# The rotary halves by a shuffle instead of a second projection, and the first prototype step inside the perceptron's slots

## The reference, cut to what matters

```
# L0: self attention with rotary q and k, cross attention, perceptron, each gated
x_norm = _ln(x, norm1_w) * (1 + sc_msa) + sh_msa
q, k, v = x_norm @ qkv_W            # 16 heads of 8 features
q, k = t * cos + rot(t) * sin       # rot(t) = concat([-t2, t1]) of a head's two halves
x = x + g_msa * (attn(q, k, v, mask) @ attn_out_W)
x = x + g_x * cross_attention(x, ctx);  x = x + g_mlp * mlp(x)
# L1: routed experts over prototypes
nx = layernorm(x) * gamma + beta
weights = softmax((nx @ Wq) @ (ctx @ Wk).T / sqrt(128))
evidence = weights @ (ctx @ Wv)
probs = softmax([nx, evidence, cond] @ router_W + router_b)
x = x + sigmoid(gate) * (sum_e probs_e * expert_e([nx, evidence, cond]) @ out_w + out_b)
# L2: cross attention; L3: self attention, cross attention, perceptron
```

## Time and profile before

| | |
|---|---|
| median of 3 runs | 1156.64 us (1152.13 to 1156.79) |
| profiled execution | 1156.29 us |
| its span in the trace | 1154.5 us |
| granted TensorE clock, mean | 0.966 |
| busy: PE, DVE, POOL, ACT | 1054.8, 783.1, 653.4, 574.2 us |
| instructions | 28612 |

### The profile page before, as it was taken

One profiled execution on the slowest core, in us unless ns is written; L12 is line 12 of the kernel. 1 busy time (PEld: TensorE's weight loads), 2 busy tenths in 40 slices (PEclk: granted clock), 3 DMA queues, 4 the chain that ended last, 5 costly groups with the idle time before them and its releaser, 6 DMA issues.

```text
span 1154.5 us, 28612 instructions
## 1 busy us (share of the span) xinstructions
PE 1054.8 (91%) x11711; PEld 665.8 (58%) x11711; DVE 783.1 (68%) x1875; ACT 574.2 (50%) x803; POOL 653.4 (57%) x762
## 2 busy tenths in 40 slices
PE   7899999999998997999899879999999999999898
PEld 4445555556654775666556545665555556665476
DVE  6677777777884433666667878878888777777321
ACT  1034444456656563544435336666556566665553
POOL 5476666677785331121112579888677665577531
PEclk8799999999999997999999979999999999999899
DMA  4300000000000112000000000000000000000001
GB/s 177 130 2 2 11 20 12 11 20 21 11 20 20 37 37 86 6 12 6 6 6 12 11 7 7 2 2 2 2 2 1 2 2 2 2 2 3 1 28 46
DMA packets 9281, 22.89 MB, mean 20 GB/s; under 512 B 1392, under 2 KB 1648, under 8 KB 8768
## 3 DMA queue, kind: packets, MB, share of 16 engines
q1 hardware_dynamic: 9152, 21.07, 5.5%
HBM read 18.90 MB, written 2.15 MB: 18 GB/s over the span
## 4 chain that ended last, share of the span: by engine, by line
PE 67%; DVE 19%; issue 6%; ACT 4%; POOL 3%; DMA 0%; DVEq 0%; POOLq 0%; ACTq 0%
PE weighed L646 11%; DVE negmax L1121 10%; PE row_scores L588 6%; PE scores L792 6%; PE weighed L669 5%; PE scores L619 5%; PE scores L545 4%; PE row_scores L792 3%; PE quads L529 3%; PE quads L552 2%; PE quads L540 2%; ACT p L1527 2%; PE scores L659 2%; PE scores L631 2%; DVE hat L1077 2%
## 5 line engine op out<-in xcount | busy, mean ns | idle before, releaser
L1121 DVE TENSOR_REDUCE negmax<-row_scores 128x8 f32<-128x616 f32 (+1 forms) x312 | 300.6, 964 | 83.7 <-PE row_scores L588 61.2
L1527 ACT ACTIVATE p<-scores 128x1024 f32<-128x1024 f32 (+1 forms) x256 | 247.6, 1018 | 214.9 <-PE scores L631 214.9
L619 PE MATMUL scores<-qblk,work 32*77 32x512 f32 (+1 forms) x1280 | 204.8, 616 | 10.5 <-ACT p L1527 5.8
L1679 POOL TENSOR_TENSOR kblk_r<-work,pack_const 128x308 fp32r<-128x308 f32 (+1 forms) x160 | 133.8, 837 | 119.5 <-PE row_scores L588 101.2
L588 PE MATMUL row_scores<-kblk_r,qr 32*128 32x308 f32 (+1 forms) x624 | 140.5, 439 | 40.0 <-DVE negmax L1121 39.0
L646 PE MATMUL weighed<-p,v 77*32 77x128 f32 (+1 forms) x5120 | 174.3, 277 | 2.5 <-DVE nat L1137 2.5
L1669 POOL TENSOR_TENSOR qblk<-work,pack_const 128x512 f32<-128x512 f32 x160 | 166.1, 1038 | 0.0
L646 PEld LDWEIGHTS weighed<-p,v 77*32 77x32 f32 (+1 forms) x5120 | 131.1, 110 | 46.2 <-issue 42.8
L631 PE MATMUL scores<-nblk,select 32*77 32x512 f32 (+1 forms) x640 | 155.3, 799 | 0.0
L588 PEld LDWEIGHTS row_scores<-kblk_r,qr 32*128 32x128 f32 x624 | 63.0, 187 | 158.2 <-issue 73.2
L1137 DVE STREAM_TRANSPOSE nat<-weighed 128x256 f32<-128x256 f32 x160 | 71.1, 444 | 45.1 <-PE weighed L646 45.1
(11 more groups left out here) (294 smaller groups left out, 1846.9 us busy)
## 6 DMA issues: line engine op xcount, KB each, us to landing
shared<-gates_hbm SPq DMA_DIRECT2D x24, 256.0 KB, 3.3
shared<-in_ctx_tok SPq DMA_DIRECT2D x16, 154.0 KB
pack_w_l<-in_w_l SPq DMA_DIRECT2D x1, 2058.5 KB, 10.9
x<-in_x_tok SPq DMA_DIRECT2D x8, 256.0 KB, 6.5
out_x<-x SPq DMA_DIRECT2D x8, 256.0 KB, 2.0
layers_w<-in_w_l SPq DMA_DIRECT2D x1, 1289.0 KB, 9.2
ctxT<-in_ctxT SPq DMA_DIRECT2D x1, 1232.0 KB, 9.1
layers_w<-in_w_l SPq DMA_DIRECT2D x1, 640.0 KB, 6.0
```

The costliest lines, as they stand in the source:

```text
L619: mm = e.matmul(scores[0:nk, g, :], k_of[q % 3][at, s * nk:(s + 1) * nk], qblk[n % 2][at, :], start=layer.mask != "qk", stop=False, skip_g ...
L1121: e.tensor_reduce(negmax[q % 2][:, 2 * h:2 * h + 2, 0, s * NJ:(s + 1) * NJ], row_banks(n, h)[:, :, 0:NJ * nk].rearrange("p g (j k) -> p g ...
L1527: e.activation(p[n % 2][0:nk, 8 * h:8 * h + 8, :], scores[0:nk, 2 * h:2 * h + 2, :].rearrange("p g (j q) -> p (g j) q", j=NJ), ACT.Exp, bi ...
L1679: e.tensor_tensor(kblk_r[n % 2][:, 0:NJ * nk].rearrange("p (j k) -> p j k", j=NJ), k_of[q % 3][:, s * nk:(s + 1) * nk].unsqueeze(1).to_bro ...
```

## The change

**Rotation.** The swapped projections and their weights go. `rotate` takes the cosine product from `quad_bank` first, then copies `quad_bank` with the two halves of each head exchanged into `rot` by `stream_shuffle` (partition i reads partition i xor 4, within 32). POOL's `add_rotated` multiplies `rot` by the sine in place, and then adds. PE's waits for the swapped result are gone.

**First prototypes.** The chain of quad 0 leaves `routed()` and gets places in the tail slots 11 to 17 of phase 0 on PE, DVE and ACT. `routed_x(0)` and `routed_x(1)` on POOL stand in slots 11 and 15, the former ahead of `add_perceptron`; quad 1's keys are projected in slot 17. The context tokens of quad 0 get a tile of their own (`ctx_first`), loaded early. The perceptron's temporary is moved out of `p[0]`, and `routed()` begins at i = 1.

```diff
-                if layer.rope:
-                    w.wait_ge(exp_done, early)
-                    e.matmul(scores[:, 1, :], W["l0_qswap"], xn[q % 3], start=True, stop=True).then_inc(proj_swapped, 1)
                 e.matmul(quad_bank[:, :], W[layer.wq], xn[q % 3], start=True, stop=True).then_inc(proj_q, 1)
...
-                w.wait_ge(proj_swapped, 2 * q + which + 1)
-                e.tensor_tensor(by_seq(rot[which][:, :]), by_seq(scores[:, 1, :]),
-                                sin_live[:, live:live + 1, :].to_broadcast([128, QUAD, S]), ALU.mult).then_inc(rope_half, 1)
-                w.wait_ge(proj, q + 1)
                 e.tensor_tensor(by_seq(dst), by_seq(quad_bank[:, :]),
                                 cos_live[:, live:live + 1, :].to_broadcast([128, QUAD, S]), ALU.mult).then_inc(rope_half, 1)
+                w.wait_ge(rope_done, 2 * (q - 1) + which + 1)
+                e.stream_shuffle(rot[which][:, :], quad_bank[:, :], [i ^ (HD // 2) for i in range(TILE)]).then_inc(rope_half, 1)
...
                 w.wait_ge(rope_half, 4 * q + 2 * which + 2)
+                e.tensor_tensor(by_seq(rot[which][:, :]), by_seq(rot[which][:, :]),
+                                sin_live[:, which:which + 1, :].to_broadcast([128, QUAD, S]), ALU.mult).then_inc(rope_turned, 1)
+                w.wait_ge(rope_turned, 2 * q + which + 1)
                 e.tensor_tensor(dst, dst, rot[which][:, :], ALU.add).then_inc(rope_done, 1)
...
+            def first_prototypes(slot):
+                if slot == 11:
+                    w.wait_ge(exp_done, 16 * NB)
+                    w.wait_ge(wo_read, 2 * NB)
+                    w.wait_ge(fold_done, FOLDING)
+                    project_keys(0)
+                if slot == 12:
+                    turn_nx(0)
+                if slot == 13:
+                    prototype_scores(0)
+                if slot == 14:
+                    turn_weights(0)
+                if slot == 15:
+                    w.wait_ge(ln_done, A_NORMS)
+                    evidence(0)
+                if slot == 17:
+                    evidence_logits(0)
+                    project_keys(1)
...
+                        if t == 4 * hi + 13:
+                            softmax_max(0)
+                            softmax_divide(0)
+                        if t == 4 * hi + 17:
+                            routed_stats(2)
+                            router_max(0)
...
+            def first_prototypes(slot):
+                if slot == 11:
+                    take_keys(0)
+                if slot == 12:
+                    take_nx(0)
+                if slot == 14:
+                    e.preload_act_table_set("natural_log_exp_and_others")
+                    w.wait_ge(r_sub, 1)
+                    e.activation(weights[0], weights[0], ACT.Exp).then_inc(r_exp, 1)
+                    routed_root(1)
+                    take_weights(0)
+                if slot == 15:
+                    take_evidence(0)
+                if slot == 17:
+                    take_keys(1)
...
-            for i in range(NB + 2):
+            for i in range(1, NB + 2):
```

More of the change, by code:

```diff
@@ L266, in build @@
               + [p_ for p_, _ in PACKS] + [f"x{c}" for c in range(NB)]
-              + [f"g{i}" for i in range(2)] + [f"ctx_tok{i}" for i in range(3)]}
+              + [f"g{i}" for i in range(2)] + ["ctx_first"] + [f"ctx_tok{i}" for i in range(3)]}
         pack_of = {name: p_ for p_, items in PACKS for name, _ in items}
@@ L459, in build @@
         mlp_banks, mlp_out_bank = [scores[:, 2, :], scores[:, 3, :], row_scores[:, 0, :], row_scores[:, 1, :]], av_bank[:, :]
-        mlp_t = [four(i, 0) for i in range(2)]
+        mlp_t = [four(1, i) for i in range(2)]
         def tensor_program(e):
@@ L520, in xn_ready, with project_q @@
                     w.wait_ge(ln_done, NORM_OF[layer.name, q].index + 1)
-            def project_q(q, early):
+            def project_q(q):
                 layer = layer_of(q)
@@ L536, in project_k @@
                     w.wait_ge(ld["ctx"], 16)
-                if layer.rope:
-                    w.wait_ge(exp_done, early)
-                    e.matmul(scores[:, 1, :], W["l0_kswap"], kv_source(q), start=True, stop=True).then_inc(proj_swapped, 1)
                 e.matmul(quad_bank[:, 0:QUAD * layer.nk], W[layer.wk], kv_source(q), start=True, stop=True).then_inc(proj_k, 1)
@@ L732, in quad_work @@
                     if cl == 3 and qi + 3 in quads:
-                        project_q(qi + 3, early)
+                        project_q(qi + 3)
                 for t in range(4 * lo + first, end):
@@ L772, in attention @@
                         turn_max(qi + 1)
+                    if phase == 0 and last is None:
+                        first_prototypes(t - 4 * hi)
                     if t == -10:
@@ L874, in routed @@
             def routed():
[L876 to L878 removed]
                 w.wait_ge(mlp_act, 4 * NB)
                 w.wait_ge(mlp_read, NB)
[L881 to L883 removed]
+                for i in range(1, NB + 1):
                     c, m = i - 1, i - 2
@@ L1402, in output_biases @@
                 done.then_inc(bias_done, 1)
-            w.wait_ge(mlp_added, NB)
-            for i in range(NB + 1):
+            for i in range(1, NB + 1):
                 c, m = i - 1, i - 2
@@ L1559, in mlp_hidden @@
-            def mlp_hidden(phase, c, hi):
-                func, bias, in_done, out_done, act_done = (
-                    (ACT.Gelu_apprx_tanh, "l0_b1", mlp_in, mlp_out, mlp_act), (ACT.Gelu, "l3_b1", ffn_in, ffn_out, ffn_act))[phase]
-                w.wait_ge(scores_done, 4 * hi)
-                for f in range(4):
-                    w.wait_ge(in_done, 4 * c + f + 1)
-                    w.wait_ge(out_done, c - 1)
-                    e.activation(mlp_h[c % 2][f], mlp_banks[f], func, bias=W[bias][:, f:f + 1]).then_inc(act_done, 1)
@@ L1833, in sync_program @@
             w.wait_ge(mlp_delta, NB)
-            for use in range(2 * NB):
+            for use in range(1, 2 * NB):
                 if use == 3:
```

178 lines of the change are left out of this document (91 added, 87 removed).

## The result

| | before | after |
|---|---|---|
| median | 1155.18 us (4 runs, 1152.13 to 1156.79) | 1138.43 us (4 runs, 1136.52 to 1139.70) |
| profiled execution, span | 1156.29, 1154.5 us | 1136.52, 1134.7 us |
| granted clock, mean | 0.966 | 0.967 |
| busy PE, DVE, POOL, ACT | 1054.8, 783.1, 653.4, 574.2 us | 1039.2, 782.1, 673.5, 571.8 us |

What follows compares the result with a forecast made beforehand. PE was taken to bound the rotary and perceptron slots, with a bare chain behind them. Rotary slots -9.6, lead -0.5 and routed start -12.6 sum to -22.7 us on 1156.29: 1133.6 us, range 1127 to 1144.

Steps and rivals of the forecast that it cites:

- Start of the routed stage: After the perceptron: quad 0's bare prototype chain, moved into perceptron slots, finds cover and the hidden layer's clock rises; -12.6 us.
- 0.78 us absorbed: Ahead of the last second layer: logits and second keys fill PE's wait for DVE, cutting moved work from 4.4 to 3.6 us.
- the hidden layer at full clock: Start of the routed stage: the first hidden layer's four records take 1.72 us instead of 3.08, another 1.4 us gained.
- Swapped projections: Rotary slots: eleven projections removed from PE, five q and six k, each worth 0.96 us; 10.6 us in all.
- DVE late by 0.20 us in each q slot: Rotary slots: the shuffle ends after PE is ready, in five q slots, giving 1.0 us back.
- Lead: Before the first slot: later spread of k against q projections saved; -0.5 us, with 3 us either way.
- The first spread of k: In the lead, where PE waits on it: POOL's two added multiplications less an earlier start cost +1.5 us.
- The two later q projections: In the lead, at half clock: their removal brings -1.1 and -0.9 us after POOL and DVE take some back.
- POOL as the bound: Rival, chance 0.12: POOL bounds the rotary slots, so only 1 us of the 9.6 is won; 1142.2 us.
- chain stalled in the slots: Rival, chance 0.08: the prototype chain stalls in perceptron slots, two waits of 3.54 us laid bare; 1140.7 us.
- the clock in the lead: Rival, chance 0.06: with five projections fewer in the lead, PE's clock rises two slots later, costing 6 us; 1139.6 us.
- Slower than before: Rival, chance 0.02: a shuffle of 3.0 us or more undoes the gains across slots and lead; 1162.4 us.

Runs made afterwards that it cites:

- e2: The kernel before with only the first prototypes moved into the perceptron's slots, old rotation and swapped projections kept: 1144.07 us, ratio 0.9892 to the kernel before.
- e8: The changed kernel with the first prototype weights' transposes right behind the scores in slot 13, no second layer between: 1142.81 us, ratio 0.9890 to the kernel before.
- e12: The changed kernel with the old rotation for the lead's five rotations (q of quads 0 to 2, k of 0 and 1): 1134.11 us, ratio 0.9813.
- e6: The changed kernel with a second, unread projection with plain weights on PE in the eleven rotary slots: 1145.56 us, ratio 0.9924 to the kernel before.
- a0: The changed kernel run again, unaltered: 1136.13 us against 1156.18 for the kernel before, ratio 0.9838.
- e1: The changed kernel with the new rotation alone, quad 0's prototype chain back in `routed()`: 1150.44 us, ratio 0.9953 to the kernel before.
- e4: The changed kernel with POOL's sine product made a second time, unread, in the slots' eleven rotations: 1147.28 us, ratio 0.9935 to the kernel before.
- e9: The changed kernel with the first three sine products on DVE and 18 unread matmuls in phase 0's lead: 1133.86 us, ratio 0.9815 to the kernel before.

## Why the prediction was right, and where it was off

**Start of the routed stage: right.** Forecast -12.6, measured -12.7 between the anchors in every profile that has the change unaltered, and -12.1 by the medians in e2. Each step held: no wait ahead of the weights, 0.78 us absorbed, the hidden layer at full clock. e8 shows that the second layer behind the scores is what covers the softmax.

**Swapped projections: right mechanism, mis-sized.** The term "11 x 0.96 = 10.6 us" took the start-to-start distance within a pair. What counts is the pair against a single one, 1.92 - 1.06 = 0.86, and the trace of before had no single one. Eleven make 9.5.

**DVE late by 0.20 us in each q slot: mis-sized, it is 0.02.** PE is ready for the spread of the maxima only 0.86 us sooner and not 0.96, so 0.10 of the 0.20 was never there. DVE starts that spread 0.08 us late, and its steps up to the end of the maximum take 0.06 less than before. 1.0 us was charged, 0.1 came. The two errors nearly cancel, and that is luck: from the first q projection of the slots to the end of the stretch, ten projections, 8.5 us came off (133.48 to 125.00), 0.85 each.

**Slot 0: not in the prediction.** The eleventh projection brought nothing. From the first mask scores to the first q projection before took 18.71 us, after 18.85, with one projection less. The last q rotation of the lead runs into this slot. Before, DVE made its sine product while PE was in the second projection. Now the product and the shuffle both stand behind one projection, and the slot's maxima stand behind them. DVE's timeline of the changed kernel (mask scores at 57.91) and of e12, where this rotation is the old one (mask scores at 56.54):

```profile
59.82 1.22 DVE L1132 TENSOR_REDUCE negmax<-row_scores 128x8 f32<-128x1024 f32 x1
```

```profile
57.83 1.21 DVE L1150 TENSOR_REDUCE negmax<-row_scores 128x8 f32<-128x1024 f32 x1
```

The maxima start 1.91 us behind the mask scores, in e12 1.29 and before 1.28. PE's next row scores start 3.27 us behind them, in e12 and before 2.64: 0.63 us lost. The shuffle of the slot's k rotation costs another 0.30 us of waiting in the next slot, in e12 too. The half clock that reaches into the slot (the mask scores take 0.94 us in place of 0.60) is not the cause: in e6 they take 0.63, and the row scores still come after 3.28. With 9.5 - 0.1 - 1.0 the stretch comes to its 8.4.

**Lead: "-0.5 us" has two terms wrong.** The first spread of k is 1.9 to 2.2 us later (e12) where 1.5 was forecast, since the product costs 1.27 and not 1.04, and the sum after it 1.41. The two later q projections were put at -1.1 and -0.9. In the first pair of profiles each brings the whole of its half-clock length, 1.71 and 1.61 us (3.55 to 1.84 and 3.45 to 1.84 from start to the next step). But between them PE loses 1.67 us (20.86 to 22.53). There stand the waits of 1.01 and 1.02 us for POOL shown above, which a0 has too (0.96 and 1.02), and a later wait for a maximum shrinks from 2.76 to 1.41. So the rows say that POOL's product is paid a second time in the lead, though no run isolates it. The first of these projections starts 1.77 us later, which gives 1.8 - 1.7 + 1.7 - 1.6 = +0.1 us in place of -0.5. The size for other executions stays open within some 3 us: with -8.4 for the slots and -12.7 for the routed start taken off, the medians leave +4.3 us (first comparison), +1.0 (a0) and +2.7 (e1) for the rest. The clock in the lead differs between executions of the same code: the first mask scores of the changed kernel came at 57.91 and 59.11 us.

**Rivals.** POOL as the bound did not come. It was not far: e4's second product finds room for 8.8 of its 14 us only. No chain stalled in the slots. The third, the clock in the lead, cannot be told from what differs between executions: the granted clock up to 57.8 us is 0.79 before, 0.74 and 0.76 in the changed kernel. Slower than before needed a shuffle of 3.0 us; it takes 0.73.

**What it adds up to.** Of the 22.7 us the profiled execution has 19.8: 1.3 are missing in the slots, 0.6 in the lead, 1.2 by chance at 362 us, and 0.2 elsewhere go the other way. The median of the first comparison is 1.9 us above its own profiled execution, that of a0 2.0 below, which is how far chance moves this kernel.

## What to carry to other kernels

A stage that stands bare can cost twice, once for its waits and once for the clock it loses (2.94 + 1.6 us in e8; in e4 three of five waits of 1.4 us cost another 1.6 each). Here moving such a chain between long, independent pieces of PE work brought 12.7 us, and eleven projections less in a full stretch 8.4. The price of one instruction out of a pair is the pair minus a single one, not the distance between the two. Idle time of an engine is room only for what can be queued ahead of the thing it waits for: POOL had 3.2 us idle per quad, and of 2.5 us more it took 1.6. When an operation is replaced by one that reads a later result, look for the places where the old one ran beside that result's making: in slot 0 the new order cost 0.6 us.

## What was not expected of the hardware

- The granted clock differs between executions of one kernel at the same instruction behind the same wait: 1.23 us of waiting, then 3.62 us for four records or 1.98 (the changed kernel and a0). The Trainium skill (TensorE: Matmul & The Clock Gate, "The HAM clock gate") says of the ramp at kernel start that it varies from run to run; here it shows deep inside the kernel too.
- PE busy without a break does not by itself bring the clock back at once: 4.00 of 4.00 us busy in each of the three windows from 42 to 54 us in e9, all at 0.50. What brings it back is not known from these runs.
- Each shuffle brings a LOAD_MASK_SELECT of 0.01 us: nothing. The shuffle reads PSUM and writes SBUF at 0.73 us for 128x512, 0.04 to 0.05 more than a product of the same size (0.68 to 0.69).
- On POOL a product of 128x512 costs 1.04 us where an operand is repeated along the innermost axis (spreads, norm steps) and 1.27 us for the sine table, which is repeated over the sequences, outside of it. Some rows with DVE work beside them are longer (1.41 and 1.50). No run tested it alone.
